# Q, K and V of a graph attention layer as three fp32r products of split operands, with GpSimd splitting the weights

## The reference, cut to what matters

```
q = (z @ Wq + bq).reshape(L, H, D)
k = (z @ Wk + bk).reshape(L, H, D)
v = (z @ Wv + bv).reshape(L, H, D)
scores = einsum('ehd,ehd->eh', q[row], k[col]) * scale + bias
alpha = softmax of scores over the edges of one row
out = segment_sum(alpha[:, :, None] * v[col], row) @ Wo + bo
```

## Time and profile before

| | |
|---|---|
| median of 3 runs | 393.78 us |
| span of the profiled execution | 394.1 us |
| TensorE matmuls busy | 374.8 us (95%) |
| VectorE busy | 312.1 us (79%) |
| ScalarE busy | 171.6 us (44%) |
| GpSimd busy | 4.2 us (1%) |
| granted TensorE clock, mean | 0.992 of full speed |

### The profile page before, as it was taken

The page is one execution under the profiler, slowest core; times in us unless marked ns, Lnnn a source line. Parts: engine busy times, 40 slices in busy tenths (PEclk is TensorE's granted clock), DMA queues, the critical chain, the costliest instruction groups (busy, mean ns, idle before and its releaser), DMA issues.

```text
span 394.1 us, 5108 instructions
## 1 busy us (share of the span) xinstructions
PE 374.8 (95%) x1786; PEld 282.2 (72%) x1786; DVE 312.1 (79%) x660; ACT 171.6 (44%) x287; POOL 4.2 (1%) x19
## 2 busy tenths in 40 slices
PE   2989999999999999999999999999999999999994
PEld 1545566666657888887678788887588878787773
DVE  5889999999848789897868976698875788388236
ACT  5664666563044234244559533262363530145410
POOL 4000000000000000000000000000000000000000
PEclk9999999999999999999999999999999999999988
DMA  7602444343135000068200512200600050000002
GB/s 238 250 1 69 152 154 141 105 153 112 52 112 183 1 2 0 2 215 315 111 2 1 172 43 101 114 0 0 211 4 0 2 180 33 2 0 0 2 12 94
DMA packets 16360, 32.92 MB, mean 84 GB/s; under 512 B 1360, under 2 KB 1488, under 8 KB 16336
## 3 DMA queue, kind: packets, MB, share of 16 engines
q1 hardware_dynamic: 15744, 32.25, 23.9%
q10 hardware_dynamic: 592, 0.36, 0.3%
HBM read 21.07 MB, written 1.05 MB: 56 GB/s over the span
## 4 chain that ended last, share of the span: by engine, by line
PE 77%; DVE 14%; ACT 4%; issue 2%; DMA 1%; DVEq 0%; ACTq 0%
PE acc L1395 11%; PE bank L1377 10%; PE bank L1480 7%; PE bank L1270 6%; PE bank L1271 6%; PE bank L1251 4%; PE acc L1251 4%; PE acc L1271 4%; PE acc L1270 4%; PE bank L1465 3%; PE acc L1451 3%; DVE big_rounded L652 2%; PE acc L1228 2%; PE bank L1228 2%; PE acc L1545 2%
## 5 line engine op out<-in xcount | busy, mean ns | idle before, releaser
L1395 PE MATMUL acc<-wide_rounded,c_rounded 128*126 128x512 f32 x200 | 59.5, 439 | 0.7 <-ACT acc L464 0.7
L1395 PEld LDWEIGHTS acc<-wide_rounded,c_rounded 128*126 128x126 f32 x200 | 36.9, 186 | 19.8 <-issue 13.0
L792 DVE TENSOR_SCALAR wide_rounded<-iota_f,picked 128x512 fp32r<-128x512 f32 x100 | 42.2, 480 | 1.5 <-issue 1.1
L483 ACT COPY z_sb<-acc 126x512 f32<-126x512 f32 x37 | 21.6, 585 | 42.0 <-PE acc L1395 33.3
L507 ACT ACTIVATE wide<-wide,low_col 128x512 f32<-128x512 f32 x32 | 21.3, 715 | 32.9 <-DVE low_col L905 32.8
L1480 PEld LDWEIGHTS bank<-v_sb,big 128*128 128x128 f32 x256 | 29.7, 192 | 4.7 <-issue 4.0
L625 DVE TENSOR_TENSOR wslot_rounded<-wslot,wide_rounded 128x512 fp32r<-128x512 f32 x24 | 16.2, 687 | 21.2 <-ACT wslot L377 21.2
L1480 PE MATMUL bank<-v_sb,big 128*128 128x65 f32 x256 | 31.6, 277 | 0.0
L798 DVE TENSOR_TENSOR c_rounded<-row_bc,wslot_rounded 128x1008 fp32r<-128x1008 bf16 x25 | 30.0, 1201 | 0.0
L1377 PE MATMUL bank<-t_sb,wslot 128*128 128x512 f32 x64 | 29.5, 594 | 0.5 <-ACT t_sb L459 0.5
L652 DVE TENSOR_TENSOR big_rounded<-big,big_rounded 128x1024 fp32r<-128x1024 f32 x24 | 29.1, 1221 | 0.5
(11 more groups left out here) (312 smaller groups left out, 769.6 us busy)
## 6 DMA issues: line engine op xcount, KB each, us to landing
big<-z_sb SPq DMA_DIRECT2D x36, 252.0 KB
big<-in_w SPq DMA_DIRECT2D x4, 2048.0 KB, 7.8
x_sb<-in_x SPq DMA_DIRECT2D x8, 256.0 KB, 4.6
big<-in_w_3t SPq DMA_DIRECT2D x2, 1024.0 KB, 6.7
row_bc<-in_rows SPq DMA_DIRECT2D x7, 256.0 KB, 6.4
wslot<-in_wq SPq DMA_DIRECT2D x1, 1024.0 KB, 8.9
wslot<-in_wk SPq DMA_DIRECT2D x1, 1024.0 KB, 10.7
wslot<-in_wv SPq DMA_DIRECT2D x1, 1024.0 KB, 12.8
```

The source lines that it names most:

```text
L483: nc.scalar.copy(stage[0:BROWS, b % STAGES, :], a).then_inc(S["staged"], 1)
L792: nc.vector.tensor_scalar(hot_ring[:, u, k, :], iota_f[:, :], picked[:, 0, s0 + k:s0 + k + 1], None, ALU.is_equal)
L1395: last = nc.tensor.matmul(to, st_ring[:, u, 2 * k + a, :, :].rearrange("p w k -> p (w k)"), hot_ring[:, u, k, :], start=False, stop=False, ...
```

## The change

- **Products.** z, transposed, is split into a rounded part `tz_hi` and a rest (in `t_sb_r`), and each of the weights into a rounded part and a rest. A step is no longer one fp32 matmul but three fp32r matmuls; a tile is 12: high by high, high by low, low by high, over four k each. There are 48 steps as before, in the same groups.
- **Order.** V comes first, then Q, then K. The first two V tiles are interleaved by part, and lie in banks 6 and 7. TensorE waits for each t tile by itself: the rounded ones at the first part, the rests (`t_lo`) at the third.
- **ScalarE** makes four rounded t tiles from PSUM, then three whole ones; the clearing of bank 3 waits for a whole tile 0, which VectorE makes from the same bank, behind `slot_weights(5, later)`.
- **VectorE** then subtracts the four rounded tiles from the whole ones (t_lo), ahead of loading the trip count and of the build of group 2.
- **GpSimd** splits Wv, Wq and Wk, each with one copy of 128 x 2048 and one subtraction of 128 x 2048 (`in_two`): Wv when it has landed, Wq when it has landed and the four h tiles are made (its high part goes to x's place), Wk when the four V products are done. From group 8 to 23 (`HELPED`) it builds the left sides of the last two slots of a group, 504 elements, and VectorE only those of the first two. TensorE waits for GpSimd ahead of a helped group's third slot.
- **Loads.** Wv is the first weight to be loaded; Wq and Wk follow in four transfers each, in columns of 128, so that their rows in memory are read in runs of 512 bytes.
- **Q and K come out** over their own weights' parts.

The diff, cut to its core:

```diff
+OWN = 2
+HELPED = range(8, NG - 1)
...
-        q_hi, q_lo, k_lo = x_sb_r, q_t_r, k_t_r
-        k_hi = wslot_r[:, 0, :, :]
+        wq_m, wk_m, wv_k = wslot[:, 0, :, :], wslot[:, 1, :, :], wslot[:, 2, :, :]
+        q_hi, q_lo = x_sb_r, wslot_r[:, 0, :, :]
+        k_hi, k_lo = q_t_r, wslot_r[:, 1, :, :]
+        wv_hi, wv_lo, tz_hi = q_t_r, wslot_r[:, 2, :, :], k_t_r
...
+        V_TILES = range(NT)
+        qkv_bank = [bank[b] for b in (6, 7, 4, 5) + 2 * (4, 5, 6, 7)]
...
-            sp.dma_start(wslot[:, 0, :, :], k_major(wq)).then_inc(S["wq_in"], 16)
-            sp.dma_start(wslot[:, 1, :, :], k_major(wk)).then_inc(S["wk_in"], 16)
-            sp.dma_start(wslot[:, 2, :, :], k_major(wv)).then_inc(S["wv_in"], 16)
+            sp.dma_start(wv_k, k_major(wv)).then_inc(S["wv_in"], 16)
             sp.dma_start(row_bc[:, 0, :], rows[0:1, :].partition_broadcast(P)).then_inc(S["bv_in"], 16)
+            for m in range(NT):
+                sp.dma_start(wq_m[:, m, :].rearrange("p (k c) -> p k c", c=P), k_major(wq)[:, :, m * P:(m + 1) * P]
+                             ).then_inc(S["wq_in"], 16)
...
+            def in_two(name, weight, hi, lo):
+
+                nc.gpsimd.tensor_copy(hi[:, :, :], weight).then_inc(S[name + "_hi"], 1)
+                pool.wait_ge(S[name + "_hi"], 1)
+                nc.gpsimd.tensor_tensor(lo[:, :, :], weight, hi[:, :, :].bitcast(F32), ALU.subtract
+                                        ).then_inc(S[name + "_lo"], 1)
+
+            pool.wait_ge(S["wv_in"], 16)
+            in_two("wv", wv_k, wv_hi, wv_lo)
+            pool.wait_ge(S["wq_in"], 16 * NT)
+            pool.wait_ge(S["h_ready"], NT)
+            in_two("wq", wq_m, q_hi, q_lo)
+            pool.wait_ge(S["wk_in"], 16 * NT)
+            pool.wait_ge(S["qkv_mm"], NT)
+            in_two("wk", wk_m, k_hi, k_lo)
+            pool.wait_ge(S["w_hi"], 2)
+            pool.wait_ge(S["round_steps"], 9)
+            for n, g in enumerate(HELPED):
+                pool.wait_ge(S["pair_mm"], (g - RING) * GROUP + GROUP + 1)
+                to, at, by = sides(g % RING, g * GROUP, OWN, GROUP - OWN)
+                nc.gpsimd.tensor_tensor(to, at, by, ALU.mult).then_inc(S["built_pool"], 1)
...
+            z_turned(0, tz_hi, "t_hi")
+            z_turned(1, tz_hi, "t_hi")
+            act.wait_ge(S["t_hi"], 1)
+            act.wait_ge(S["t_ready"], 1)
+            clear(Z_BANKS[0])
+            z_turned(2, tz_hi, "t_hi")
+            z_turned(3, tz_hi, "t_hi")
+            for t in range(1, NT):
+                z_turned(t, t_sb, "t_ready")
...
             dve.sem_inc(S["weights_read"], 1)
+            dve.wait_ge(S["cols_in"], 16)
+            dve.wait_ge(S["t_hi"], 1)
+            nc.vector.tensor_scalar(t_sb[:, 0, :], bank[Z_BANKS[0]][:, :], colp("ln1_g", 0), colp("ln1_b", 0),
+                                    ALU.mult, ALU.add).then_inc(S["t_ready"], 1)
             build(1, 1, GROUP)
...
+            for t in range(NT):
+                dve.wait_ge(S["t_hi"], t + 1)
+                dve.wait_ge(S["t_ready"], t + 1)
+                nc.vector.tensor_tensor(t_sb_r[:, t, :], t_sb[:, t, :], tz_hi[:, t, :].bitcast(F32), ALU.subtract
+                                        ).then_inc(S["t_lo"], 1)
...
-                build(g, g % RING, g * GROUP, (g - RING) * GROUP)
+                build(g, g % RING, g * GROUP, (g - RING) * GROUP, OWN if g in HELPED else GROUP)
...
-                ins = nc.tensor.matmul(to[:, :], left, right, start=(k == 0), stop=(k == NT - 1))
+                for n, i, k, left, right in qkv[3 * step:3 * step + 3]:
...
+                    ins = nc.tensor.matmul(qkv_bank[n][:, :], left, right, start=(i == 0 and k == 0),
+                                           stop=(i == 2 and k == NT - 1))
...
+                    if k == OWN and type(g) is int and g in HELPED:
+                        pe.wait_ge(S["built_pool"], g - HELPED[0] + 1)
...
                 if g == 0:
+                    pe.wait_ge(S["weights_read"], 1)
+                if g == 1:
                     pe.wait_ge(S["t_ready"], NT)
-                if g == 1:
-                    pe.wait_ge(S["weights_read"], 1)
```

More of the change, by code:

```diff
@@ L1364, in pair_table, with qkv_tile @@
                 last.then_inc(S["weights_mm"], 1)
-            qkv = [(bank[4 + t], tile(wslot[:, 0, k, :], t), t_sb[:, k, :], k) for t in range(NT) for k in range(NT)]
-            qkv += [(bank[4 + t], tile(wslot[:, 1, k, :], t), t_sb[:, k, :], k) for t in range(NT) for k in range(NT)]
-            qkv += [(bank[4 + t], tile(t_sb[:, k, :], t), wslot[:, 2, k, :], k) for t in range(NT) for k in range(NT)]
-            def qkv_step(n):
-                to, left, right, k = qkv[n]
-                if n % (NT * NT) == 0:
-                    pe.wait_ge(S[("wq_in", "wk_in", "wv_in")[n // (NT * NT)]], 16)
-                if k == 0 and n >= NT * NT:
-                    pe.wait_ge(S["qkv_ready"], n // NT - NT + 1)
-                ins = nc.tensor.matmul(to[:, :], left, right, start=(k == 0), stop=(k == NT - 1))
-                if k == NT - 1:
-                    ins.then_inc(S["qkv_mm"], 1)
+            def qkv_tile(n):
+                t = n % NT
+                if n in V_TILES:
+                    left = [(tile(tz_hi[:, k, :], t), tile(t_sb_r[:, k, :], t)) for k in range(NT)]
+                    right = [(wv_hi[:, k, :], wv_lo[:, k, :]) for k in range(NT)]
+                    parts = ((0, 0), (0, 1), (1, 0))
+                else:
+                    hi, lo = (q_hi, q_lo) if n < 2 * NT else (k_hi, k_lo)
+                    left = [(tile(hi[:, t, :], k), tile(lo[:, t, :], k)) for k in range(NT)]
+                    right = [(tz_hi[:, k, :], t_sb_r[:, k, :]) for k in range(NT)]
+                    parts = ((0, 0), (0, 1), (1, 0))
+                return [(n, i, k, left[k][a], right[k][b]) for i, (a, b) in enumerate(parts) for k in range(NT)]
@@ new lines, in _, with qkv_step @@
+            first, second = qkv_tile(0), qkv_tile(1)
+            qkv = [p for i in range(3) for tiles in (first, second) for p in tiles[i * NT:(i + 1) * NT]]
+            qkv += [p for n in range(2, 3 * NT) for p in qkv_tile(n)]
+            LAST_STEP = 4 * 3 * NT - 1
+            def qkv_step(step):
+                for n, i, k, left, right in qkv[3 * step:3 * step + 3]:
+                    name = ("wv", "wq", "wk")[n // NT]
+                    if n % NT == 0 and k == 0:
+                        if i == 0:
+                            pe.wait_ge(S[name + "_hi"], 1)
+                        if i == (1 if n in V_TILES else 2):
+                            pe.wait_ge(S[name + "_lo"], 1)
+                    if n == 0 and i in (0, 2):
+                        pe.wait_ge(S["t_lo" if i else "t_hi"], k + 1)
+                    if i == 0 and k == 0 and n >= NT:
+                        pe.wait_ge(S["qkv_ready"], n - 1 if n < NT + 2 else n - NT + 1)
+                    ins = nc.tensor.matmul(qkv_bank[n][:, :], left, right, start=(i == 0 and k == 0),
+                                           stop=(i == 2 and k == NT - 1))
+                    if i == 2 and k == NT - 1:
+                        ins.then_inc(S["qkv_mm"], 1)
```

72 lines of the change are left out of this document (36 added, 36 removed).

## The result

| | before | after |
|---|---|---|
| median of the runs | 393.81 us (393.72 to 395.19, 4 runs) | 409.14 us (407.08 to 410.87, 4 runs) |
| ratio | | 1.0373, 95% interval 1.0341 to 1.0405 |
| span of the profiled execution | 394.1 us | 405.3 us |
| first exponential of the attention | 116.74 us | 129.82 us |
| from there to the end of the span | 277.4 us | 275.5 us |

A forecast was written before the change was run, and what follows sets the result against it. TensorE and VectorE were taken as nearly co-bound, with TensorE alone in the chain of waits. 8.0 - 0.6 - 0.3 - 1.0 = 6.1 us gained, 393.78 - 6.1 = 387.7 us; 8-in-10 range 385.5 to 404.

The forecast's parts named there:

- TensorE's part: Q, K and V products: three fp32r matmuls save 0.167 us a step, 8.0 us in all if TensorE sets the pace.
- GpSimd's part: Weight splits and half left sides: copies 3 us, subtractions 4.5, halves 1.2, all hidden if GpSimd and VectorE don't disturb each other.
- Rival A: GpSimd blocks VectorE's fast single-input or two-SBUF-input operations: about 413 us in full (chance 0.12), 402 in part (0.22).
- VectorE's pace: Group builds: groups 4 to 7 lose 0.3 us; from group 8, with GpSimd's help, 2.53 us against TensorE's 2.55.
- The start: Before the first products and early builds: 0.5 us gained, 0.5 waited, late builds and masks 0.6; net 0.6 us lost.
- Tail: Last two tiles become K, not V, costing VectorE 1.45 instead of 0.68 us each: 1.0 us lost, ends 0 and 1.6.
- The time outside the span: Whole run: profiled span 394.1 us, the runs' median 393.78, 0.3 below it; the forecast starts from the median.
- The range: Whole kernel time, for 8 in 10: 385.5 to 404 us, leaving out Rival A in full and the tips.

The follow-up runs named there:

- kernel 1: The change with GpSimd's three weight splits and sixteen half left sides cut to two elements each, products reading a constant tile: 392.09 us, ratio 0.9930.
- Kernel 3: The change with only GpSimd's three weight splits cut to two elements, half left sides kept in full: 395.80 us, ratio 1.0038.
- kernel 2: The change with all left sides on VectorE again, GpSimd still splitting the weights in full: 409.48 us, ratio 1.0357.
- kernel 4: The change with the weight splits cut to two elements and all left sides on VectorE: 394.54 us, ratio 1.0017.
- kernel 7: kernel 1 with wq's split at full size, begun when VectorE begins its four t_lo subtractions: 395.40 us, ratio 1.0008.
- kernel 6: kernel 1 with four staging tiles for the blocks' rows in place of three: 390.43 us, ratio 0.9875.
- kernel 9: The kernel before the change with four staging tiles in place of three: 393.80 us, ratio 0.9988.
- kernel 8: The change with wv's split begun behind the first two one-hots, GpSimd's 2048-element instructions cut in four, six groups helped: 403.00 us, ratio 1.0204.

## Why the prediction was wrong, step by step

- **TensorE's part (8.0 us):** right in size. From group 6 on in kernel 1 a group's pairs start 3.22 to 3.35 and then 2.53 to 2.56 us after the last wherever TensorE doesn't wait, by the forecast's 1.86 plus 1.38 or 0.69. In the change itself it is never seen, since VectorE sets the pace.
- **GpSimd's part:** the sizes were right or on the safe side, 1.9 to 2.1 us for a copy of 2048 (3 forecast), 4.5 to 4.7 for a subtraction (4.5), 1.08 for a half (1.2). **The step that failed is "All these are zero as durations, if GpSimd and VectorE don't disturb each other".** The condition does not hold. The cover named, slack between the parts' landing and their use, was real and beside the point: the cost is not that the parts are late but that VectorE stands still. Kernel 3, the change with light splits, has its first exponential 11.1 us earlier. Of these 7.7 lie ahead of the one-hots of group 1 (31.30 against 23.62 us: transposes 6.3 later, 1.4 for their lower clock). The other 3.4 are, in the main, what reached the end of the 5.4 us for which wk's split held VectorE; the halves stand beside one-hots in both kernels.
- **Rival A was right in mechanism and too low in chance.** I gave 0.34 to both of its forms, though the one row that could test it, the 0.75 us copy, spoke for it. (The prediction's "no row shows a reading GpSimd instruction" goes too far: the selects of the earlier trace rows read. None of them ran beside a VectorE operation.) Its prices: start 9 (here 7.7), wk 5 (a stop of 5.4, of which 3.4 arrived), helped groups 9 (such a group took 3.01 us, not 3.7, and against kernels 2 and 4 the help cost 0.5 to 1.6 us in all). The last was too dear since a half holds VectorE for 0.8 us and saves it 0.53, and in five of the sixteen groups it stood beside a way out and was free. So 409.14 lies between its 402 and 413. The coefficient operation of which it spoke did wait, 4.25 us, but in kernel 2's profiled execution and not in the change's. The Trainium skill's rule (SBUF — State Buffer, Who interferes with whom: an exclusive lock, held by whoever came first for the whole instruction, wanted by VectorE's two-port modes and, against a GpSimd instruction that reads, by operations with two SBUF inputs) agrees with the rows above on who stops whom: one-hots, left sides and the operation of four elements stopped, the moments and the ways out of PSUM not, GpSimd in its turn held by left sides and subtractions. On who goes first the rows say more than "whoever came first". In kernel 7 the copy began behind the first of four subtractions and ended as if all four had gone ahead of it. Wk's copy in the change began at 51.17 beside one-hots and ended at 54.42; less the 1.9 us that it takes alone that is 52.5, about where the left sides ended (52.66), though these had begun after it, at 51.46. The starts that the profile gives for GpSimd are rough, so this is read from few rows.
- **VectorE's pace:** "1.58 + 0.59 + 0.36 = 2.53" was wrong. Its first two terms, a helped group without its share of a tile, are 2.17; such a group takes 91.14 - 88.13 = 3.01 us, from one start of its one-hots to the next, where an unhelped one takes 2.70. The help makes it slower unless a way out is beside it.
- **The start (0.6 us lost):** under-sized. The forecast counted VectorE's subtractions and not ScalarE's three more t tiles with the blocks' way out behind them. The quicker TensorE then finds three staging tiles full and banks uncleared: 1.9 us by kernels 1 and 6, hidden in the kernel before by kernel 9. What the three t tiles cost by themselves was not tried.
- **Tail (1.0):** too dear. From the last pairs to the first exponential it is 8.05 us before and 8.28 after, so 0.2.
- **The time outside the span:** "the runs' median 393.78, 0.3 below" the span of 394.1 compared two executions of different length. A run of before lasts 1.5 us longer than its own span (393.83 against 392.3), and the profiled execution was one of the longer kind. It did not move the forecast, which starts from the median.
- **The range** held 385.5 to 404; 409.14 lies outside, because A in full and its upper tip had been cut.

## What to carry to other kernels

Before you hand work to GpSimd as "free", list what VectorE executes in that window. In these traces it was free beside single-input statistics and reads from PSUM; beside the one-hots and beside operations with two SBUF operands its duration, or most of it, was VectorE's too. A split of work is worth it only if what it takes off VectorE is more than the time that it holds it; here 1.08 us of GpSimd saved 0.53 and cost 0.8. When an engine gets faster, look at the queue behind it that it used to hide (here three staging tiles), and test the cover itself with one kernel in which the hidden work is made tiny.

## What the runs showed that I had not expected

- An instruction of two elements on GpSimd can take 1.3 us where its own work is 0.18, when VectorE holds the shared path (kernel 1: the copies took 0.18 and 0.18, the third, begun beside one-hots, 1.31). The duration that a profile gives for a GpSimd instruction is therefore not always its work.
- Cutting GpSimd's instructions in four made the total longer (wk's copy and subtraction 10.5 us in kernel 8, 7.9 in the change), as if GpSimd now waited for VectorE between the pieces, and VectorE's stop hardly changed: its two groups there took 6.1 us longer, of which some 0.8 belong to the half that follows, in place of 5.4 in one.
- A late layer norm cost twice: 6.2 us of waiting, and 1.4 us more since TensorE's clock had fallen while it was idle (granted 0.50 from 24 us on, with nothing on TensorE since 18.3).
- The stretch behind the first exponential comes in two lengths, some 275.5 and 277.2 us, over the fourteen profiled executions; in the kernel before the longer one has a granted clock of 0.86 from 370 to 380 us, and so, at 0.71 to 0.91 in windows of some 5 us, have the other longer ones. What sets it off stayed open.
